# First-half read sums of the experts phase moved from GpSimd to TensorE and ScalarE, and two experts' weight loads put ahead of the front tile's store

## What is computed

```python
xn = _layernorm(x)
# attention part: a gated delta rule with 16 heads of 16 x 16 state, run over the 512 tokens
def step(S, (q, k, v, b, g)):
    S = S * g
    S = S + b * outer(k, v - k @ S)
    o = q @ S                      # the read: a sum over the 16 key channels
    return S, o
a = xn + out @ Wo + bo
a = a + mlp(_layernorm(a))
# mixture of experts: 64 experts, 8 of them per token, 128 tokens at most each, and a shared one
y = segment_sum(weight * (silu(xb @ w_gate) * (xb @ w_up)) @ w_down) + shared(xn)
return x + a + y
```

## Time and profile before

| what | value |
|---|---|
| median of 3 runs | 1865.07 us (1864.67 to 1867.93) |
| the profiled execution's own time | 1868.96 us |
| its span, first to last instruction | 1866.9 us |
| mean granted TensorE clock, of full speed | 0.855 |
| VectorE busy | 1693.1 us, 91% |
| GpSimd busy | 1591.9 us, 85% |
| TensorE busy | 1422.3 us, 76% |
| ScalarE busy | 810.6 us, 43% |

### The profile page before, as it was taken

The page is one execution under the profiler, slowest core; times in us unless marked ns, Lnnn a source line. Parts: engine busy times, 40 slices in busy tenths (PEclk is TensorE's granted clock), DMA queues, the critical chain, the costliest instruction groups (busy, mean ns, idle before and its releaser), DMA issues. The chain is left out here.

```text
span 1866.9 us, 31499 instructions
## 1 busy us (share of the span) xinstructions
PE 1422.3 (76%) x8846; PEld 1231.1 (66%) x8846; DVE 1693.1 (91%) x4988; ACT 810.6 (43%) x2548; POOL 1591.9 (85%) x1354
## 2 busy tenths in 40 slices
PE   6776777877863677575666559898998999889858
PEld 5665666766753576464655548777776877768647
DVE  3699999999999999899977989998999999899980
ACT  4534454545444544345432235444543453334313
POOL 5379999899998889888897789999999999999961
PEclk9978878878875887777877669998999999989889
DMA  8674234533346657846667422242223311211110
GB/s 182 167 167 122 70 100 118 142 83 98 93 117 166 158 135 177 214 107 172 147 155 212 102 52 61 68 127 83 72 56 106 90 57 49 66 50 56 46 46 22
DMA packets 337169, 201.24 MB, mean 108 GB/s; under 512 B 208226, under 2 KB 327716, under 8 KB 336996
## 3 DMA queue, kind: packets, MB, share of 16 engines
q1 hardware_dynamic: 318724, 168.43, 34.7%
q0 software_dynamic: 15616, 30.55, 7.3%
q10 hardware_dynamic: 2656, 0.26, 0.1%
HBM read 127.58 MB, written 71.60 MB: 107 GB/s over the span
## 5 line engine op out<-in xcount | busy, mean ns | idle before, releaser
L846 POOL TENSOR_TENSOR rp<-S,qs 128x2048 f32<-128x2048 f32 x113 | 521.2, 4612 | 43.1 <-DVE S L1169 29.6
L1169 DVE SCALAR_TENSOR_TENSOR S<-S,gwin,bank 128x256 f32<-128x256 f32 x1024 | 496.6, 485 | 0.3
L1159 DVE TENSOR_REDUCE nu<-vwin 128x16 f32<-128x272 f32 x1024 | 451.5, 441 | 0.3
L1163 DVE TENSOR_TENSOR bank<-nu,bank 128x256 f32<-128x256 f32 x1024 | 443.5, 433 | 0.6
L1154 DVE TENSOR_TENSOR vwin<-S,bank 128x256 f32<-128x256 f32 x1024 | 434.8, 425 | 0.0
L854 POOL TENSOR_TENSOR r<-rp 128x1024 f32<-128x1024 f32 x113 | 273.6, 2421 | 7.0
L1510 ACT ACTIVATE region<-bank,b_s 128x128 f32<-128x128 f32 x512 | 144.8, 364 | 274.1 <-PE bank L1821 274.1
L1821 PEld LDWEIGHTS bank<-region 128*128 128x128 f32 x2048 | 247.6, 200 | 21.5 <-issue 16.2
L1821 PE MATMUL bank<-region 128*128 128x128 f32 x2048 | 260.0, 287 | 2.2 <-ACT region L1500 2.2
L1701 PE MATMUL bank<-xaT,wqkvg 128*128 128x128 f32 (+1 forms) x1792 | 240.5, 287 | 23.1 <-ACT xaT L1355 19.9
L1701 PEld LDWEIGHTS bank<-xaT,wqkvg 128*128 128x128 f32 (+1 forms) x1792 | 215.0, 189 | 37.3 <-ACT xaT L1355 23.9
(11 more groups left out here) (170 smaller groups left out, 2285.4 us busy)
## 6 DMA issues: line engine op xcount, KB each, us to landing
qkv_d<-stg SPq DMA_DIRECT2D x192, 128.0 KB, 3.1
region<-in_L_ffn_w_gate SPq DMA_DIRECT2D x64, 192.0 KB, 3.9
region<-in_L_ffn_w_up SPq DMA_DIRECT2D x64, 192.0 KB, 4.1
region<-in_L_ffn_w_down SPq DMA_DIRECT2D x64, 192.0 KB, 4.9
region<-in_L_attn_x SPq DMA_DIRECT2D x16, 512.0 KB, 7.3
region<-in_L_attn_x SPq DMA_DIRECT2D x32, 256.0 KB, 4.4
xw_d<-region SPq DMA_DIRECT2D x32, 256.0 KB, 4.0
acc_d<-region SPq DMA_DIRECT2D x32, 256.0 KB, 4.0
```

The lines of the kernel that those rows point to most:

```text
L846: g.tensor_tensor(rp[:, :, :].rearrange("p (a v) d -> p a v d", v=DH), S[h][:, lo:lo + HS].rearrange("p t s (v d) -> p (t s) v d", v=DH), ...
L1159: m[G] = mark(v.tensor_reduce(nu[:, G], products_of(I, s, G)[1], AX.X, ALU.add))
L1163: m[G] = mark(v.tensor_tensor(outer[G].rearrange("p (v d) -> p v d", v=DH), nu[:, G].unsqueeze(2).to_broadcast([P, DH, DH]), key(L, s, G), ...
L1169: ins = v.scalar_tensor_tensor(S[h][:, s, G], earlier(h, s, G), gwin[:, I // NB2 & 1, G, 1, t:t + 1], outer[G], ALU.mult, ALU.subtract)
```

## The change

The change touches iterations `on_tensor(I)`: 19 to 33 without j 7, thirteen of them. In these GpSimd's `reads` of the first half ends behind the product rp and scatter 0. One iteration later TensorE adds the 16 key channels (`read_rows`): sixteen products with the identity, each of which reads one channel of rp, a moving operand with a step of 16 elements, accumulate into `rsum`, the last quarter of the bank LG. They stand between the transpose of expert 2's input and the front tile's q and k. ScalarE copies rsum into oblk (`rows_out`) behind its copy of expert 2's input. New waits keep the buffers apart: GpSimd's next product into rp waits for TensorE's sums, TensorE's next slot products and sums for ScalarE's copy, GpSimd's store of oblk for that copy too; GpSimd's `products` and ScalarE's copy wait for the last store of oblk.

On SyncE the weights of the first iteration are loaded as before. Those of each later one are issued at the end of the iteration before: experts 0 and 1 ahead of the next window's loads and of the front tile's store, experts 2 and 3 behind it.

```diff
+def on_tensor(I):
+    return X0 <= I < X1 - 1 and I % NB2 != NB2 - 1
+
+def tensor_sums_before(I):
+    return sum(on_tensor(i) for i in range(I))
...
+        rsum = LG[:, 3 * P:4 * P]
...
-            def experts(n):
-                for r in range(RT):
+            def experts(n, turns):
+                for r in turns:
...
-                if X0 <= I < X1:
-                    experts(I - X0)
+                if I == X0:
+                    experts(0, range(RT))
...
+                if X0 <= I < X1 - 1:
+                    experts(I - X0 + 1, (0, 1))
                 if I >= R1 and j < 2 and I // NB2 + 1 < NBLK:
                     next_window(I // NB2, j)
                 if I >= R1 and f is not None:
                     front_store(f, f // NB2, f % NB2, h)
+                if X0 <= I < X1 - 1:
+                    experts(I - X0 + 1, (2, 3))
...
                 pool.wait_ge(act_staged, I + 1)
+                pool.wait_ge(row_sums[0], tensor_sums_before(I))
...
                 if mid_work is not None:
                     mid_work()
+                if half == 0 and on_tensor(I):
+                    return
...
                 pool.wait_ge(x_sums, 2 * sums_before(I))
+                pool.wait_ge(o_stored, (I >> 3) * OST)
...
                     pool.wait_ge(x_sums, 2 * sums_before(I))
+                    pool.wait_ge(row_out[0], tensor_sums_before(I))
...
+            def rows_out(I, half):
+                act.wait_ge(row_sums[half], tensor_sums_before(I) + 1)
+                act.wait_ge(o_stored, (I >> 3) * OST)
+                t0 = I % NB2 * ST + half * HS
+                a_.activation(oblk[:, :, :, t0:t0 + HS], rsum.rearrange("p (t s v) -> p s v t", s=2, v=DH), ACT.Copy).then_inc(row_out[half], 1)
...
                 unit_evac(q + 2)
+                if on_tensor(I - 1):
+                    rows_out(I - 1, 0)
                 front_qk(f, h)
...
+            def read_rows(I):
+
+                pe.wait_ge(prod_done, I * 2 + 3)
+                pe.wait_ge(slot_used, min(I + 1 - R1, NR))
+                pe.wait_ge(row_out[0], tensor_sums_before(I))
+                for d in range(DH):
+                    last = mm(rsum, ident[:, :], rp[:, :, d], start=(d == 0), stop=(d == DH - 1))
+                last.then_inc(row_sums[0], 1)
...
                 expert_T(n, q + 2, 2, hx)
+                if on_tensor(I - 1):
+                    read_rows(I - 1)
                 front_qk(f, h)
                 if t < NR:
+                    pe.wait_ge(row_out[0], tensor_sums_before(I))
                     slot_round(t)
```

More of the change, by code:

```diff
@@ L367, in layer @@
         act_staged = sem("act_staged")
-        rec_done = sem("rec_done"); x_sums = sem("x_sums"); prod_done = sem("prod_done"); o_stored = sem("o_stored")
+        rec_done = sem("rec_done"); x_sums = sem("x_sums"); row_sums = [sem(f"row_sums{n}") for n in range(2)]; row_out = [sem(f"row_out{n}") for n in range(2)]; prod_done = sem("prod_done"); o_stored = sem("o_stored")
         x4_ld = [sem(f"x4_ld{i}") for i in range(BUF)]; xn_ready = sem("xn_ready"); t_done = sem("t_done")
```

## The result

| | before | after |
|---|---|---|
| median of the timed runs | 1866.05 us (1864.67 to 1867.93, 4 runs) | 1877.88 us (1875.55 to 1879.47, 4 runs) |
| profiled execution, its span | 1868.96, 1866.9 us | 1877.34, 1875.2 us |
| experts phase, VectorE's iterations 19 to 36 | 497.9 us | 519.0 us |
| behind it, iterations 36 to 63 | 692.2 us | 683.4 us |

The ratio is 1.0056, 95% interval [1.0038, 1.0075]. The forecast was 1842 us with a range up to 1864: the time lies outside, on the other side of no change. It is the first rival, the slower one, that came true.

A forecast was written before the change was run, and what follows sets the result against it. The prediction took GpSimd to bound the experts phase by VectorE's 35.0 us of waits: 1868.96 - 35.0 + 18 (TensorE) - 5.2 (next phase's entry) - 3.9 (profile to median), forecast 1842 us, range 1820 to 1864.

The forecast's parts named there:

- the first rival, the slower one: TensorE becomes the bound: the sixteen products take 6.0 us or more; time 1875 to 1890, chance 0.15.
- so I take 4.0: TensorE's sixteen added f32 products per iteration, 32 records, were to take 4.0 us at the upper clock level.
- TensorE's price: Longer loop through TensorE and ScalarE in the experts phase: 18 us of new VectorE waits, bounds nothing to 59.
- the row that spoke for 8.0: Two bf16 products began 0.10 us apart with a 132-byte step, 0.05 with adjacent elements; that factor gives 8.0 us, 1887 in sum.
- GpSimd's relief: Thirteen iterations lose the first half's sums on GpSimd, 3.09 us each, 40.2 in all; VectorE's 35.0 us of waits go.
- the third rival: GpSimd stays the bound because successive scatters land slower than 4.56 us; at spacing 7.65 the time is 1860; chance 0.12.
- Most scatters in the phase wait for no landing: Reason for taking the upper bound, 40.2 us, of GpSimd's relief in the experts phase.
- New waits, where they stand: VectorE's waits per iteration: ordinary 0.9 us, behind squares 1.8, behind norms 3.8, iteration 25 3.1, 33 and 34 nothing.
- GpSimd's new wait, booked at nothing: GpSimd's wait before rp for TensorE's read of the iteration before: no cost, unless TensorE is late there.
- ScalarE's copy, nothing: Copy of the sums, 0.4 us per iteration, hidden while TensorE does q and k; otherwise 5 us in all.
- The weights, nothing: Experts 0 and 1 loaded ahead of the front tile's store: no gain by itself, cover for the later front tile.
- The entry of the next phase, -5.2: VectorE's 2.78 and 2.45 us waits in iterations 36 and 37 go as GpSimd is less late; bounds 0 to 10.

The follow-up runs named there:

- e1: Changed kernel, but TensorE's sixteen products read adjacent elements of rp, so other elements are summed: 1846.77 us, ratio 0.9883 to the kernel before.
- e10: Changed kernel, but GpSimd writes the product channel by channel so TensorE reads adjacent elements, sums kept; second run: 1844.70 us, ratio 0.9880.
- e2_gap: Changed kernel with the sixteen products, step kept, moved into TensorE's idle stretch behind an iteration's first transposes: 1843.22 us, ratio 0.9875.
- e8_gap_no0_apart: Changed kernel, sixteen products in TensorE's idle stretch, only in eleven iterations, GpSimd's product written channel by channel: 1844.09 us, ratio 0.9862.
- e3: Changed kernel with all four experts' weights in their old place behind the front tile's store: 1882.53 us, ratio 1.0084.
- e9: Changed kernel with TensorE reading adjacent elements of rp, GpSimd's write unchanged, other elements summed; run again: 1844.49 us, ratio 0.9879.
- e5: Kernel before with only the new order of weights, two experts' ahead of the front tile's store: 1864.04 us, ratio 0.9969.
- e11: Changed kernel with the sixteen stepped products in TensorE's idle stretch, run again on another occasion: 1840.93 us, ratio 0.9855.
- e6_apart: Changed kernel, but GpSimd writes the product channel by channel so TensorE reads adjacent elements, sums kept; first run: 1862.64 us, ratio 0.9964.

## Why the prediction was wrong

**The step that failed: "so I take 4.0" for the sixteen products.** It is the term of TensorE's price, mis-sized: 7.13 us measured. The prediction's own formula, with 7.13 in place of 4.0 in 11 iterations, gives 18 + 11 x 3.1 = 52 us of new waits, and 55.3 were measured; the sum becomes 1868.96 - 35.0 + 52.4 - 5.2 - 3.9 = 1877.3, against a median of 1877.88. The closeness is in part luck: the waits of those 11 iterations were 50.2 us, and 4.9 more stood in iteration 33, booked at nothing; GpSimd's relief, the weights and the stretch behind the phase were off too, as said below. By all four runs of before 2.9 comes off for the median, not 3.9. e1 and e10 show the reverse: with 3.7 us the waits are 18.4 and 15.4 and the times 1846.8 and 1844.7, close to the 1842 forecast.

**Why 4.0 was taken against the row that spoke for 8.0.** The earlier trace rows had the factor 2 for a step of 132 bytes, and it was set aside because "f32 takes two passes per product and so asks for fewer elements per us". The premise holds: at the upper level (granted clock 1.00) a record of f32 moves its 128 columns in 3.74 us / 32 = 0.117 us, 0.91 ns per column, while eight bf16 records of 66 adjacent columns begin 0.22 / 7 = 0.031 us apart, 0.5 ns per column. Before, the first and the last of the eight:

```profile
890.63 0.19 PE L1851 MATMUL bank<-region 128*128 128x66 bf16 x1
...
890.85 0.19 PE L1852 MATMUL bank<-region 128*128 128x66 bf16 x1
```

The conclusion doesn't follow, and the prediction missed that both pairs of the earlier trace rows ran at the lower level (granted clock 0.50). What stays the same across the rows is not a factor but the time per column of a stepped read: 0.10 us / 64 = 1.6 ns for bf16 at the lower level, 7.13 / 32 / 128 = 1.74 ns for f32 at the upper. And for f32 at the lower level e2_gap has 17 records in 4.05 us at a granted clock of 0.50, 0.23 us each, 1.8 ns per column. All 32 of them, in TensorE's timeline of e2_gap:

```profile
990.54 7.32 PE L1922 MATMUL bank<-rp,ident 128*128 128x128 f32 x32 [6.65 <-POOL rp L860]
```

And the reads of adjacent elements in e8_gap_no0_apart:

```profile
876.31 5.96 PE L1923 MATMUL bank<-rp,ident 128*128 128x128 f32 x32 [0.18 <-issue]
...
620.77 3.81 PE L1923 MATMUL bank<-rp,ident 128*128 128x128 f32 x32 [0.39 <-issue]
```

The mean granted clocks of the three are 0.61, 0.62 and 1.00. With the step 32 records take 7.1 to 7.3 us at either level; with adjacent elements they take 3.8 at the upper level, and at the lower 16 records alone took 3.73, so 32 some 7.5. So the step doubles the time at the upper level and costs nothing that can be seen at the lower. Read as a time per column, the pair of the earlier trace rows gives 32 x 128 x 1.6 ns = 6.4 us for the sixteen, above the 6.0 from which the slower rival decides. It is one pair of another type and step, so this is a fair estimate and no more.

The Trainium skill ("SBUF — State Buffer", section "Specifications (TRN2)") has the rule that each access into a new 16-byte line costs a penalty. At the upper level the traces agree in direction: 128 adjacent f32 lie in 32 such lines, 128 with a step of 64 bytes in 128, and the record took 0.223 us instead of 0.117, a factor of 1.9 for four times the lines. At the lower level, 0.23 us with either operand, no penalty is seen. The rule was weighed and had no chance of its own beside the slow rival's 0.15; by the only row of its kind it deserved the larger share.

**The other steps.**
- *GpSimd's relief:* the waits went as forecast, but the relief was mis-sized. VectorE's 35.0 us of waits for GpSimd are gone, in e3 and e10 too, and in e1 up to 2.3. The spacing of scatters 0 and 1 over the thirteen iterations of after was 5.62 us on average (4.90 to 6.25; a usual one below), not 4.56. By the prediction's own formula the relief was then 13 x (7.65 - 5.62) = 26 us, not 40.2, and less than the 35.0 needed. This is the condition of the third rival, and as that one says it changes nothing as long as VectorE waits for TensorE anyway: GpSimd has play behind the slower loop. GpSimd's timeline in after:

```profile
676.77 1.59 POOL L907 DMA_INDIRECT acc_d<-region,idx_i  x1 [0.15 <-issue]
...
682.29 1.56 POOL L907 DMA_INDIRECT acc_d<-region,idx_i  x1 [3.93 <-DMA acc_d<-region,idx_i]
```

- *"Most scatters in the phase wait for no landing":* so it was before, and it didn't carry over. The waits of after list 48.3 us in 13 waits for the landing of the scatter before; with the sums gone, it is what bounds the second scatter.
- *New waits, where they stand:* right in the main. In all they were 6.4 and 6.7 us behind norms, 3.7 to 5.6 behind squares, 7.5 in iteration 25 behind a window's first one, and 2.7 to 3.6 in the ordinary iterations. But iteration 33, also behind a window's first one, had 4.9 where nothing was forecast. Of the iterations at 677 us (behind norms), 800 (iteration 25) and 895 (behind squares), VectorE's timeline of after:

```profile
677.10 0.42 DVE L1112 TENSOR_TENSOR hg_s<-sgu,bank 96x256 f32<-96x256 f32 x1 [5.14 <-ACT sgu L1465]
...
799.72 0.42 DVE L1112 TENSOR_TENSOR hg_s<-sgu,bank 96x256 f32<-96x256 f32 x1 [6.95 <-ACT sgu L1465]
...
894.73 0.42 DVE L1112 TENSOR_TENSOR hg_s<-sgu,bank 96x256 f32<-96x256 f32 x1 [3.13 <-ACT sgu L1465]
```

- *GpSimd's new wait, booked at nothing:* 11.6 us in 4 waits, the case that the prediction named (TensorE late). With 3.7 us for the sixteen it is gone (e9, e10), so it hangs on the same term.
- *ScalarE's copy, nothing:* right; the 71.6 us that it waits for TensorE are inside ScalarE's idle time until q and k are there. It took 0.28 us.
- *The weights, nothing:* off by some 5 us on the good side, as far as e3 and e5 can tell.
- *The entry of the next phase, -5.2:* the two waits of the earlier trace rows are gone in after and 8.8 us came off behind the phase. But the reason given, GpSimd less late, isn't shown. e10, in which VectorE waits for no rx either, has 690.5 us there against 692.2 before, with three waits for the MLP's banks, the first:

```profile
1117.26 0.42 DVE L1157 TENSOR_TENSOR region<-bank,region 128x256 f32<-128x256 f32 x1 [2.35 <-PE bank L1859]
```

  In after VectorE comes 20 us later, which would hide such a wait as well. Yet e2 and e11, early too, have 684. What decides between 684 and 691 is open.
- *The clock:* rather a gain. The mean granted clock rose from 0.78 to 0.86 in the phase, and the sixteen ran at the upper level, as taken. By e2_gap's rows the lower level would have made them hardly longer.

The chances were too sure: 0.15 for a rival whose price stood in the only row of its kind, and a range that ended 11 us below the slow case.

## What to carry to other kernels

Work that is moved to another engine must be priced in the layout in which it lies. A moving operand of f32 that steps over its neighbours took 1.9 times as long here at TensorE's upper clock level; laying it out otherwise at its producer cost nothing and turned +0.6% into -1.2%. When the row that is nearest in kind speaks against the sum, take its value, with the clock level at which it stood, and not an argument why it need not hold. And a long stretch of products is best put where TensorE idles anyway: 7.2 us cost nothing there in the ordinary iterations, and at its end the clock was at the upper level.

## What the runs showed of the hardware that was not expected

- A matmul record of 128x128 f32 took 275 ns with an adjacent moving operand and 394 ns with a step of 64 bytes, while 32 of them one behind the other took 3.74 and 7.13 us: the pace differs by 1.9, the record's own length by 1.4. That is at the upper level of the clock; at the lower (granted 0.50) the stepped ones kept their pace of 0.23 us, the same as adjacent ones there.
- GpSimd's product wrote its 2048 elements in another order of addresses (4972 ns in e10_apart_again) in the time of the usual one (4956 ns in e9_adjacent_again).
- Two accumulating scatters with nothing between them, the second waiting for the landing of the first, stood 5.62 us apart on average in the thirteen iterations of after (4.90 to 6.25).
- Sixteen records of gate products took 1.93 us behind the sixteen sums and 3.73 us behind an idle stretch of TensorE of 5 to 8 us.
- On one of the chips ScalarE stood still for stretches of some 3 us that nothing in the kernel ended (46.6 us in e6_apart), and the same code stood at 0.9964 of the kernel before there, at 0.9880 on a chip without them (e10_apart_again).
